# Cross attention with scores made twice: once with queries on partitions for the maximum, once with keys on partitions for the exponential, and fp32 products with the values

## The chip, the cores and the metric

The kernel runs on one core of a Trainium2 chip. The metric is the device time of one launch in microseconds (us). A core has TensorE for matrix products (PE in the profile, its weight loads PEld), VectorE (DVE), ScalarE (ACT), GpSimd (POOL) and SyncE (SP), which starts DMAs. PE writes its results to PSUM, eight banks of 2 KB on each of 128 partitions; everything else lies in SBUF. The engines run side by side and wait for one another at semaphores. PE has two clock levels, 2.4 and 1.2 GHz; the profile shows which of them was granted.

## The reference

A decoder layer on x of 64 images by 128 tokens by 128 channels: self attention, cross attention to a context of 77 keys by 96 channels, and a soft mixture of 64 experts with 32 slots, each with a residual and a layer norm. The change is in the cross attention alone, which has 16 heads of 8 channels:

```python
q = (x @ Wq).reshape(B, N, HEADS, hd).transpose(0, 2, 1, 3)
k = (context @ Wk).reshape(B, M, HEADS, hd).transpose(0, 2, 1, 3)
v = (context @ Wv).reshape(B, M, HEADS, hd).transpose(0, 2, 1, 3)
scores = jnp.einsum('bhid,bhjd->bhij', q, k) * scale
scores = jnp.where(context_mask[:, None, None, :], scores, max_neg)
attn = jax.nn.softmax(scores, axis=-1)
out = jnp.einsum('bhij,bhjd->bhid', attn, v)
out = out.transpose(0, 2, 1, 3).reshape(B, N, DIM)
return out @ Wo
...
x = _layernorm(x + _L0_xattn_ref(x, ctx_768, mask_BxS2_bf1, ...), axis=-1)
```

All values are fp32.

## The kernel before

The program is a row of stages: setup, `attention` (self attention), `attend_context` (cross attention), `prepare_slots`, `gather_slots`, `run_experts`, `mix_slots`. Each stage writes one instruction list for each engine by hand, with its own semaphores. There is no scheduler: an engine does its list in order. `steps` runs a function `step(k)` over the items, and each engine's `step` works on items k, k - 1, k - 2 and k - 3 at once, so that a stage of 32 items runs for 32 + 3 steps.

In `attend_context` an item is a pair of images, and a step has four quarters j, each for eight heads of one image (j // 2 is the image). The work for a quarter:

- Queries and keys of the pair are made once (`queries_keys`, L537 and L538), rounded to fp32r (`qkh`, L672) and the rest kept as `qkl` (L768). POOL spreads each key over four copies, each with the channels of one head only (`kbh`, `kbl`, L816). In this way a product over 32 channels gives four heads' scores side by side, 4 x 78 = 312 columns.
- `scores` (L591 to L595): two groups of four heads, each in its own 32 rows of PE's array, with three fp32r products (high by high, low by high, high by low) and one of a single row that adds the mask. Queries lie on the partitions, heads and keys on the columns.
- DVE takes the maximum over the keys of each head (L764), and `shift` (L602) subtracts it on PE by a product with the negated identity.
- ACT makes the exponential twice, in fp16 (`ph`, L699) and in fp32 (`p32`, L700), and POOL subtracts for the low part `pl` (L850).
- `turn` (L615, L616) transposes high and low part of eight heads, 16 fp16 transposes of 128 queries by 77 keys; DVE copies the high part out of PSUM (L788), ACT the low part (L690).
- `values` (L630, L631): for each head two products with the values, which were split in three bf16 parts on ACT, DVE and POOL (L676, L793, L800, L835, L840); a column of ones among them gives the sum of the exponentials.
- DVE adds the parts (L715), inverts 16 sums (L721) and multiplies (L726); PE transposes the result (L548), ACT copies it (L660), PE projects (L552), and DVE adds the residual (L731), takes the statistics (L736, L741), normalises (L746, L750), with POOL for the power (L820, L822). PE transposes again (L556), ACT and DVE keep high and low part (L664, L756).

One bank of PSUM, `psM`, serves eight small products of a step in turn. Their order, and whose reading frees the bank for the next, stands in a table that `use_bank` walks through:

```python
USES = [(queries_keys, qkl_ready, 0, None), (project, y_done, 3, 1), (own_values, v32_ready, 0, None),
        (turn_out, oT_ready, 2, 0), (project, y_done, 2, 0), (turn_x2, xl_ready, 3, 1),
        (turn_x2, xl_ready, 2, 0), (turn_out, oT_ready, 2, 1)]
```

The scores have two buffers of two banks (`psL`), the transposes one bank each, the products with the values one.

Of the kernel before, what the change touches and what calls it, by code (L numbers as in the profile page):

```python
# [18 lines left out]
ALU = mybir.AluOpType  # L19
# [25 lines left out]
C_IDENT, C_HEAD, C_END = 0, 128, 132  # L45


def constants():
    k = np.arange(128)
    c = np.zeros((128, C_END), np.float32)  # L50
    c[:, C_IDENT:C_HEAD] = np.eye(128)
    c[:, C_HEAD:C_END] = (k[:, None] % 32) // HD == np.arange(4)[None, :]
    return c
# [67 lines left out]
def setup(nc, io, w):  # L121

    with ExitStack() as ctx:
# [18 lines left out]
        def _(sync):  # L142
# [4 lines left out]
            for p in ROWS:  # L147
                sync.dma_start(w.mask[p:p + 1, :], io["mask"]).then_inc(w.mask_loaded, 16)

# [48 lines left out]
def attention(nc, io, w):  # L198
# [4 lines left out]
    with ExitStack() as ctx:  # L203
# [153 lines left out]
        def _(dve):  # L357

            dve.wait_ge(w.mask_loaded, 16 * len(ROWS))
# [87 lines left out]
def attend_context(nc, io, w):  # L447

    PAIRS = B // 2
    HW = 4 * JP
    with ExitStack() as ctx:
# [5 lines left out]
        fp = [st.sb(f"fp{i}", [128, 2, JP], BF16) for i in range(2)]  # L461
        kbh = [st.sb(f"kbh{i}", [128, 2, 4, JP], F32R) for i in range(2)]
# [5 lines left out]
        mx = [st.sb(f"mx{i}", [128, 2, 4], F32R) for i in range(2)]  # L468
        p32 = [st.sb(f"p32{i}", [128, 2, HW]) for i in range(2)]
        ph = [st.sb(f"ph{i}", [128, 2, HW], F16) for i in range(2)]  # L470
        pl = [st.sb(f"pl{i}", [128, 2, HW], F16) for i in range(2)]
        pTh = [st.sb(f"pTh{i}", [J, 8, 128], F16) for i in range(2)]
        pTl = [st.sb(f"pTl{i}", [J, 8, 128], F16) for i in range(2)]
        o9 = st.sb("o9", [128, HEADS, 9])
        orec = st.sb("orec", [128, HEADS])
        on = st.sb("on", [128, 128])
        oT = st.sb("oT", [128, 128])
# [14 lines left out]
        (qk_made, qkh_ready, qkl_ready, kbh_ready, kbl_ready, v_made, v32_ready, high_ready, rest_ready, mid_ready,  # L492
         last_ready, vs_ready) = (
            st.sem(n) for n in ("qk_made", "qkh_ready", "qkl_ready", "kbh_ready", "kbl_ready", "v_made", "v32_ready",
                                "high_ready", "rest_ready", "mid_ready", "last_ready", "vs_ready"))

        s_made, mx_ready, shifted, ph_ready, p32_ready, pl_ready, t_made, pTh_ready, pTl_ready, av_made = (
            st.sem(n) for n in ("s_made", "mx_ready", "shifted", "ph_ready", "p32_ready", "pl_ready", "t_made",
                                "pTh_ready", "pTl_ready", "av_made"))

        o_sum, o_rec, on_ready, oT_made, oT_ready, pj_made, y_done, st_done, mv_ready, ve_done, rstd_ready, x2_ready, xT_made, xh_ready, xl_ready = (
            st.sem(n) for n in ("o_sum", "o_rec", "on_ready", "oT_made", "oT_ready", "pj_made", "y_done", "st_done",
                                "mv_ready", "ve_done", "rstd_ready", "x2_ready", "xT_made", "xh_ready", "xl_ready"))
        consts_set, fp_ready = st.sem("consts_set"), st.sem("fp_ready")
        block = ctx.enter_context(nc.Block())

        def earlier(r, j, s):

            return (r, j - s) if j >= s else (r - 1, j - s + 4)


        def part(r, c):
            return vs[r.par][:, :, :, c, 0:8]
# [1069 lines left out]
```

## Time and profile before

| | us |
|---|---|
| median of 3 runs | 1877.24 (1876.05 to 1879.13) |
| the profiled execution, its span | 1877.9 |
| cross attention in it, from 191 to 757 | 566 |
| PE busy in that stretch | 494.2 |
| DVE busy | 423.5 |
| ACT busy | 348.5 |
| POOL busy | 339.6 |

The span is the time from the first to the last instruction of one execution. Busy time is the sum over an engine's instructions without overlap. A PE record lasts until its result is in PSUM, so records of products that follow each other overlap, and the distance between two starts tells what one costs. The granted clock is a share of 2.4 GHz: 1.00 is the high level throughout, 0.50 the low one throughout.

### The profile page before, as it was taken

The page shows a single profiled execution, that of the slowest core. Times are in us where ns is not written, and L with a number is a line of the kernel's source. Part 1 is how long each engine was busy: PE and PEld are TensorE (multiplying, and loading weights), DVE is VectorE, ACT ScalarE, POOL GpSimd, SP SyncE. Part 2 cuts the span into 40 slices and gives each one's busy share as a digit, 9 for nine tenths or more (in the row PEclk, how much of TensorE's full clock was granted, in tenths as well). Part 3 has the DMA queues.
Part 4 walks back from the last instruction along what each step waited for, and adds up shares of the span by engine and source line. Part 5 has one row for each costly group of instructions (what it writes and reads, how often), then busy time and mean ns, then how long its engine had stood idle before and what let it go on. Part 6 is the DMA issues. An engine that isn't in the chain of part 4 may idle for free. (4 is left out here: it accounts for less than half of the span.)

```text
span 1877.9 us, 39937 instructions
## 1 busy us (share of the span) xinstructions
PE 1659.8 (88%) x12606; PEld 1368.6 (73%) x12606; DVE 1536.8 (82%) x2882; ACT 1055.2 (56%) x2091; POOL 1307.6 (70%) x1040
## 2 busy tenths in 40 slices
PE   6775788988898898799999999879999999999997
PEld 5664577777777776577777777558888888888886
DVE  5998477778867877788888888758999999999996
ACT  2443466666656665455566555445555555555554
POOL 2333466666656655499999999817887888787887
PEclk8786688888878888899999999979999999999999
DMA  4010100000000000300000000000000000000000
GB/s 132 28 28 6 30 6 6 4 3 4 4 3 4 4 3 2 91 1 0 0 0 0 0 0 0 1 1 4 7 10 6 6 8 6 8 6 8 6 9 12
DMA packets 19980, 21.20 MB, mean 11 GB/s; under 512 B 1925, under 2 KB 14278, under 8 KB 19914
## 3 DMA queue, kind: packets, MB, share of 16 engines
q1 hardware_dynamic: 18314, 15.95, 3.1%
q0 software_dynamic: 1088, 4.19, 0.8%
q8 instruction: 35, 0.57, 0.1%
q10 hardware_dynamic: 512, 0.23, 0.0%
q14 instruction: 31, 0.25, 0.0%
HBM read 16.17 MB, written 4.19 MB: 11 GB/s over the span
## 5 line engine op out<-in xcount | busy, mean ns | idle before, releaser
L1491 POOL TENSOR_TENSOR mix_c<-mix_e,mix_rinv 128x1024 f32<-128x1024 f32 x128 | 306.9, 2397 | 151.3 <-ACT mix_rinv L1401 151.2
L1458 DVE TENSOR_REDUCE mix_sg<-mix_e 128x256 f32<-128x1024 f32 x128 | 258.5, 2019 | 43.1 <-ACT mix_e L1396 39.5
L850 POOL TENSOR_TENSOR cross_pl<-cross_p,cross_ph 128x624 f16<-128x624 f32 x128 | 175.1, 1368 | 166.0 <-ACT cross_p L700 165.9
L1064 POOL TENSOR_TENSOR gather_d<-gather_e,gather_rinv 128x1024 f32<-128x1024 f32 x128 | 245.2, 1916 | 48.9 <-DVE gather_rinv L1039 40.9
L1007 ACT ACTIVATE gather_e<-gather_L 128x1024 f32<-128x1024 f32 x128 | 131.3, 1026 | 156.5 <-PE gather_L L974 156.5
L690 ACT COPY cross_pTl<-cross_Tl 77x1024 f16<-77x1024 f16 x128 | 129.2, 1009 | 131.3 <-PE cross_Tl L616 131.3
L1029 DVE TENSOR_REDUCE gather_mx<-gather_L 128x32 fp32r<-128x1024 f32 x128 | 156.8, 1225 | 36.6 <-PE gather_L L955 30.6
L1035 DVE TENSOR_REDUCE gather_rsum<-gather_e 128x32 f32<-128x1024 f32 x128 | 156.2, 1221 | 30.9 <-ACT gather_e L1007 30.8
L1056 POOL TENSOR_TENSOR gather_dl<-gather_d,gather_dh 128x512 fp32r<-128x512 f32 x128 | 166.0, 1297 | 0.0
L1485 POOL TENSOR_TENSOR mix_cl<-mix_c,mix_ch 128x512 fp32r<-128x512 f32 x128 | 164.7, 1287 | 0.0
L1283 PE MATMUL mix_L<-kept_xh,kept_w2h 128*128 (+1 forms) x512 | 156.6, 306 | 5.9 <-DVE mix_ykl L1412 5.2
L1446 DVE TENSOR_REDUCE mix_mg<-mix_L 128x256 f32<-128x1024 f32 x128 | 154.7, 1209 | 6.9 <-PE mix_L L1285 5.1
L615 PE MATMUL cross_Th<-kept_ident,cross_ph 128*77 128x128 f16 x1024 | 159.0, 247 | 0.0
L616 PE MATMUL cross_Tl<-kept_ident,cross_pl 128*77 128x128 f16 x1024 | 158.9, 247 | 0.0
L1396 ACT ACTIVATE mix_e<-mix_L 128x1024 f32<-128x1024 f32 x128 | 131.4, 1027 | 38.0 <-PE mix_L L1294 38.0
L1284 PE MATMUL mix_L<-kept_xl,kept_w2h 128*128 (+1 forms) x512 | 145.6, 284 | 0.0
L1285 PE MATMUL mix_L<-kept_xh,kept_w2l 128*128 (+1 forms) x512 | 145.4, 284 | 0.0
L764 DVE TENSOR_REDUCE cross_mx<-cross_L 128x8 fp32r<-128x624 f32 x128 | 102.3, 799 | 44.5 <-PE cross_L L595 44.3
L616 PEld LDWEIGHTS cross_Tl<-kept_ident,cross_pl 128*77 128x77 f16 x1024 | 138.1, 138 | 0.0
L1294 PE MATMUL mix_L<-kept_neg_ident,mix_me 128*128 128x256 f32 x512 | 95.1, 308 | 46.5 <-ACT mix_me L1388 44.4
L615 PEld LDWEIGHTS cross_Th<-kept_ident,cross_ph 128*77 128x77 f16 x1024 | 135.1, 137 | 1.3 <-issue 0.3
L964 PE MATMUL slots_X<-gather_d,gather_x 128*128 128x512 f32 x256 | 134.1, 605 | 1.0 <-issue 1.0
(224 smaller groups left out, 5129.5 us busy)
## 6 DMA issues: line engine op xcount, KB each, us to landing
attn_xTg<-in_xT SPq DMA_DIRECT2D x16, 256.0 KB, 2.7
kept_xres<-in_x POOLq DMA_DIRECT2D x4, 1024.0 KB, 11.2
out<-mix_res SPq DMA_DIRECT2D x32, 128.0 KB, 1.8
cross_cg<-in_ctxT SPq DMA_DIRECT2D x32, 58.5 KB, 1.8
setup_wT<-in_w_qkvT SPq DMA_DIRECT2D x1, 192.0 KB
kept_consts<-in_consts SPq DMA_DIRECT2D x1, 66.0 KB
first_xq<-in_xq ACTq DMA_DIRECT2D x1, 64.0 KB, 2.9
setup_wproj<-in_w_proj SPq DMA_DIRECT2D x1, 64.0 KB
```

Of the source, the lines that this page charges most:

```text
L615: pe.transpose(psTh[:, h, :], ph[j % 2][:, h // 4, c], w.ident16[:])
L616: ins = pe.transpose(psTl[:, h, :], pl[j % 2][:, h // 4, c], w.ident16[:])
L850: pool.tensor_tensor(pl[j % 2][:], p32[j % 2][:], ph[j % 2][:], ALU.subtract).then_inc(pl_ready, 1)
L1029: dve.tensor_reduce(mx[j][:], psL[j][:].rearrange("p i (n s) -> p i n s", n=16), X, ALU.max)\
L1035: dve.tensor_reduce(rsum[ju][:].rearrange("p (i n) -> p i n", i=2), e[ju][:], X, ALU.add)\
L1056: pool.tensor_tensor(dl[j3][:], dd[t3.par][j3][:, 0, :], dh[j3][:], ALU.subtract)\
L1064: pool.tensor_tensor(dd[tu.par][ju][:].rearrange("p i (n s) -> p i n s", n=16), e[ju][:], rinv[ju][:].rearrange("p (i n) -> p i n", i=2).u ...
L1283: pe.matmul(o, w.w2h[:, k], w.xh[:, at], start=(c % 2 == 0), stop=False, skip_group_check=True)
L1446: dve.tensor_reduce(mg[j % 2][:], psL[j % 2][:].rearrange("p i (c t) -> p t (i c)", c=2), X, ALU.max).then_inc(mg_ready, 1)
L1458: dve.tensor_reduce(sg[j1 % 2][:], e[j1][:].rearrange("p c t -> p t c"), X, ALU.add)\
L1485: pool.tensor_tensor(cl[j5 % 2][:], cc[j5][:, 0:SPLIT, :], ch[j5 % 2][:], ALU.subtract)\
L1491: pool.tensor_tensor(cc[j3][:], e[j3][:], rinv[j3 % 2][:].unsqueeze(1).to_broadcast([128, 4, 256]), ALU.mult)\
```

## The change

The scores of a pair are still made with queries on the partitions, but only for the maximum. They are made a second time with the keys on the partitions; the negated maximum is added there, the exponential is taken once in fp32, and its output is at once the moving operand of the product with the values.

- A step has two halves b, one for each image, and the lag of the stage is 2 steps and not 3. `scores` is called for the two halves of the heads of one image, into one buffer `psS`.
- DVE writes the 16 maxima of each query so that a head's maximum lies in column 32 g + i (g is the group of four heads, i the head in it). `turn_max` is one fp32r product with the negated identity, ACT copies it to `mT`.
- `turned_scores`: 48 fp32r products of 32 rows (channels) by 77 columns (keys) as weights and 128 moving columns (queries), in the order of the four 32-row groups g, and 16 products with a 0/1 selector `pick` that add the negated maximum of each head to its scores.
- ACT: two exponentials of 77 x 1024 for each image, with the mask as a bias for each partition.
- `values` and `sums`: 16 plain fp32 products each, weights of 77 rows by 32 columns (in `vd` the eight channels of one head stand in their place and the rest is zero, in `od` ones stand there), 128 moving columns, in the order of the four 32-column groups. The output has channels on the partitions, so the transpose of the output is no longer needed.
- DVE inverts 128 x 128 sums out of PSUM and multiplies 128 x 128.
- The exponential's low part, both copies of transposes, the three-way split of the values and `shift` are gone.

```diff
-        v32 = st.sb("v32", [J, 256])
-        vr = [st.sb(f"vr{i}", [J, 256]) for i in range(2)]
-        vs = [st.sb(f"vs{i}", [J, 2, HEADS, 3, 9], BF16) for i in range(2)]
...
+        vd = [st.sb(f"vd{i}", [J, 8, 160]) for i in range(2)]
+        od = st.sb("od", [J, 160])
+        mx = [st.sb(f"mx{i}", [128, 128], F32R) for i in range(2)]
+        pick = st.sb("pick", [128, 4, JP], F32R)
+        mT = st.sb("mT", [128, 128], F32R)
+        pT = st.sb("pT", [J, 4, 4, 128])
...
-        psL = [st.ps(f"L{i}", [128, 2, 512]) for i in range(2)]
-        psTh = st.ps("Th", [J, 8, 128], F16)
-        psTl = st.ps("Tl", [J, 8, 128], F16)
-        psA = st.ps("A", [128, 512])
+        psS = st.ps("S", [128, 2, 512])
+        psP = st.ps("P", [J, 4, 4, 128])
+        psO = st.ps("O", [128, 2, 128])
...
+            def turn_max(r, b):
+                pe.wait_ge(mx_ready, r.after(4, 2 * b + 2))
+                pe.matmul(psM[:, 0:128], mx[b][:], w.neg_ident[:], start=True, stop=True).then_inc(m_made, 1)
...
+            USES = [(project, y_done, 2, 0), (queries_keys, qkl_ready, 0, None), (turn_max, mT_ready, 1, 0),
...
+            def turned_scores(r, b):
+                reach(pe, e_ready, r.after(4, 2 * b))
+                bc = slice(b * 128, b * 128 + 128)
+                for h in range(4):
+                    for n, (ks, qs) in enumerate(((kbh, qkh), (kbl, qkh), (kbh, qkl))):
+                        for g in range(4):
+                            gr = slice(32 * g, 32 * g + 32)
+                            pe.matmul(psP[:, g, h, :], ks[r.par][gr, b, h, 0:J], qs[r.par][gr, bc],
+                                      start=(h == 0 and n == 0), stop=False, skip_group_check=True)
+                pe.wait_ge(mT_ready, r.after(2, b + 1))
+                for h in range(4):
+                    for g in range(4):
+                        gr = slice(32 * g, 32 * g + 32)
+                        ins = pe.matmul(psP[:, g, h, :], pick[gr, h, 0:J], mT[gr, :], start=False, stop=True,
+                                        skip_group_check=True)
                 ins.then_inc(t_made, 1)
...
+            def values(r, b):
+                if b == 0:
+                    pe.wait_ge(vd_ready, r.after(1, 1))
+                pe.wait_ge(e_ready, r.after(4, 2 * b + 2))
+                reach(pe, oT_ready, r.after(2, b))
+                for h in range(4):
+                    for g in range(4):
+                        pe.matmul(psO[32 * g:32 * g + 32, 0, :], vd[r.par][:, 4 * b + g, 32 * h:32 * h + 32],
+                                  pT[:, g, h, :], start=(h == 0), stop=(h == 3), skip_group_check=True)
...
+                        ins = pe.matmul(psO[32 * g:32 * g + 32, 1, :], od[:, 32 * h:32 * h + 32], pT[:, g, h, :],
+                                        start=(h == 0), stop=(h == 3), skip_group_check=True)
...
+                for half in range(2):
+                    hs = slice(2 * half, 2 * half + 2)
+                    act.activation(pT[:, hs, :, :], psP[:, hs, :, :], ACT.Exp, bias=fb[r.par][:, b:b + 1])\
+                        .then_inc(e_ready, 1)
...
+                dve.reciprocal(rs[:], psO[:, 1, :]).then_inc(rs_ready, 1)
...
+                dve.tensor_tensor(oT[b][:], psO[:, 0, :], rs[:], ALU.mult).then_inc(oT_ready, 1)
```

The mask comes a second time, with keys on partitions: one more small DMA in setup on SP's queue, and one DVE instruction at the start of the self attention. POOL keeps `kbh` and `kbl` and the power, and takes over the copy of the mask row (`fp`) from ACT.

How PE's list changes. This is the list of the kernel before for one quarter (eight heads, half an image); in brackets the semaphores that an instruction waits for.

```order
L591 MATMUL cross_L<-cross_kbh,cross_qkh 128x312 [waits cross_p32_ready]
...
L595 MATMUL cross_L<-cross_fp,first_ones 128x312
...
L542 MATMUL cross_M<-first_xv,cross_cg 77x128 [waits cross_y_done]
...
L630 MATMUL cross_A<-cross_vs,cross_pTh 128x27 [waits cross_pTl_ready,cross_pTh_ready,cross_o_sum]
L631 MATMUL cross_A<-cross_vs,cross_pTl 128x18
...
L615 MATMUL cross_Th<-kept_ident,cross_ph 77x128 [waits cross_pTh_ready,cross_pTl_ready,cross_pl_ready,cross_ph_ready]
L616 MATMUL cross_Tl<-kept_ident,cross_pl 77x128
...
L602 MATMUL cross_L<-cross_mx,kept_neg_ident 128x312 [waits cross_mx_ready]
L602 MATMUL cross_L<-cross_mx,kept_neg_ident 128x312
L548 MATMUL cross_M<-kept_consts,cross_on 128x128 [waits cross_on_ready,cross_v32_ready]
```

Four such blocks make a pair; the 16 products of `values`, the 16 transposes and the two of `shift` are all that is gone from a block, the scores stay.

And this is PE's list for one whole image after the change, the second of a pair. S are the scores for the maximum, M the shared bank, O the output, P the scores with keys on partitions.

```order
L579 MATMUL cross_S<-cross_kbh,cross_qkh 128x312 [waits cross_mx_ready]
...
L583 MATMUL cross_S<-cross_fp,first_ones 128x312
...
L542 MATMUL cross_M<-first_xo,cross_oT 128x128 [waits cross_oT_ready,cross_xl_ready]
L579 MATMUL cross_S<-cross_kbh,cross_qkh 128x312 [waits cross_mx_ready]
...
L532 MATMUL cross_M<-first_xv,cross_cg 77x128 [waits cross_y_done]
...
L612 MATMUL cross_O<-cross_pT,cross_vd 32x128 [waits cross_oT_ready,cross_e_ready,cross_vd_ready]
...
L538 MATMUL cross_M<-kept_neg_ident,cross_mx 128x128 [waits cross_mx_ready,cross_vd_ready]
L619 MATMUL cross_O<-cross_pT,cross_od 32x128 x16
L546 MATMUL cross_M<-kept_consts,cross_xp 128x128 [waits cross_x2_ready,cross_mT_ready]
L594 MATMUL cross_P<-cross_qkh,cross_kbh 77x128 [waits cross_e_ready]
...
L600 MATMUL cross_P<-cross_mT,cross_pick 77x128 [waits cross_mT_ready]
L600 MATMUL cross_P<-cross_mT,cross_pick 77x128 x15
```

All of an image's work up to the next image's scores now stands in one row behind the wait for the maximum: `turn_max`, the sums, the transpose of the normalised image, 48 products with keys on partitions and 16 with `pick`. The product with the values of the image before stands ahead of `turn_max`.

DVE's list of the kernel before, for the third quarter of a step, between two maxima:

```order
L731 TENSOR_TENSOR cross_y<-cross_M,kept_xres 128x128 [waits cross_pj_made]
L736 BN_STATS cross_stats<-cross_y 128x6 [waits cross_y_done]
L715 TENSOR_REDUCE cross_o<-cross_A 128x144 [waits cross_on_ready,cross_av_made]
L740 MEMSET kept_scratch 128x1 [waits cross_st_done]
L741 BN_AGGR cross_mv<-cross_stats 128x2
L788 COPY cross_pTh<-cross_Th 77x1024 [waits cross_av_made,cross_t_made]
L793 CAST cross_vs<-cross_vr 77x32x8 [waits cross_last_ready]
L746 TENSOR_SCALAR cross_xp<-cross_y,cross_mv,cross_rstd 128x127 [waits cross_xT_made,cross_rstd_ready]
L756 TENSOR_TENSOR kept_xl<-cross_M,kept_xh 128x128 [waits cross_xh_ready]
```

Here the maxima of two different buffers alternate, with two PSUM copies and the sum of the parts among the work between them.

And after the change, from the first maximum of an image to the end of its half step:

```order
L702 TENSOR_REDUCE cross_mx<-cross_S 128x2x4 [waits cross_m_made,cross_s_made]
L718 TENSOR_TENSOR cross_y<-cross_M,kept_xres 128x128 [waits cross_pj_made]
L723 BN_STATS cross_stats<-cross_y 128x6 [waits cross_y_done]
L702 TENSOR_REDUCE cross_mx<-cross_S 128x2x4 [waits cross_s_made]
L727 MEMSET kept_scratch 128x1 [waits cross_st_done]
L728 BN_AGGR cross_mv<-cross_stats 128x2
L733 TENSOR_SCALAR cross_xp<-cross_y,cross_mv,cross_rstd 128x127 [waits cross_xT_made,cross_rstd_ready]
L737 TENSOR_SCALAR kept_xres<-cross_y,cross_mv,cross_rstd 128x128
L709 RECIPROCAL cross_rs<-cross_O 128x128 [waits cross_oT_ready,cross_av_made]
L714 TENSOR_TENSOR cross_oT<-cross_O,cross_rs 128x128 [waits cross_pj_made,cross_rs_ready]
L743 TENSOR_TENSOR kept_xl<-cross_M,kept_xh 128x128 [waits cross_xh_ready]
```

The second maximum now waits for scores that PE can only make once the first maximum has read them out of the one buffer, and the inversion of the sums stands between the residual of an image and the bank's next release (`kept_xl`).

## Rows read from the trace of the kernel before

**Rows 1.** The page: busy time of each engine, share of the span.
```profile
PE 1659.8 (88%) x12606; PEld 1368.6 (73%) x12606; DVE 1536.8 (82%) x2882; ACT 1055.2 (56%) x2091; POOL 1307.6 (70%) x1040
```

**Rows 2.** By stretch: length, busy PE, PEld, DVE, ACT, POOL, clock, DMA, GB/s.
```profile
191.00:757.00 566.00, 494.16 (x5888) 409.67 (x5888) 423.51 (x991) 348.49 (x639) 339.63 (x384) 0.83 0.02 6
...
820.00:1222.00 402.00, 392.88 (x1503) 275.95 (x1502) 335.15 (x442) 233.92 (x458) 368.92 (x237) 1.00 0.00 0
...
249.00:257.00 8.00, 7.67 (x109) 6.45 (x106) 7.42 (x21) 5.91 (x10) 5.21 (x6) 1.00 0.05 10
257.00:265.00 8.00, 6.50 (x72) 4.98 (x69) 5.20 (x12) 4.84 (x11) 5.33 (x6) 0.72 0.01 2
```

**Rows 3.** One line: count, ns (min, median, max), first and last start.
```profile
L731 DVE TENSOR_TENSOR cross_y<-cross_M,kept_xres x64: 273/277/292, 224.7 to 754.4; 128x128 f32<-128x128 f32 x64
```

**Rows 4.** Lines of the cross attention: busy us, mean ns, idle before, releaser.
```profile
L850 POOL TENSOR_TENSOR cross_pl<-cross_p,cross_ph 128x624 f16<-128x624 f32 x128 | 175.1, 1368 | 166.0 <-ACT cross_p L700 165.9
...
L690 ACT COPY cross_pTl<-cross_Tl 77x1024 f16<-77x1024 f16 x128 | 129.2, 1009 | 131.3 <-PE cross_Tl L616 131.3
L764 DVE TENSOR_REDUCE cross_mx<-cross_L 128x8 fp32r<-128x624 f32 x128 | 102.3, 799 | 44.5 <-PE cross_L L595 44.3
...
L726 DVE TENSOR_TENSOR cross_on<-cross_o,cross_orec 128x128 f32<-128x128 f32 x64 | 56.9, 890 | 0.0
L746 DVE TENSOR_SCALAR cross_xp<-cross_y,cross_mv,cross_rstd 128x127 f32<-128x127 f32 x64 | 55.4, 866 | 20.9 <-POOL cross_rstd L822 19.3
...
L816 POOL TENSOR_TENSOR cross_kbh<-cross_qkh,kept_consts 128x624 fp32r<-128x624 f32 x32 | 39.3, 1228 | 25.3 <-ACT cross_qkh L672 25.3
...
L721 DVE RECIPROCAL cross_orec<-cross_o 128x16 f32<-128x16 f32 x64 | 15.3, 239 | 0.0
```

**Rows 5.** PE in order of time, clock at 2.4 GHz: start us, busy us, line.
```profile
457.73 0.17 PE L630 MATMUL cross_A<-cross_vs,cross_pTh 77*128 77x27 bf16 x1
457.75 0.17 PE L631 MATMUL cross_A<-cross_vs,cross_pTl 77*128 77x18 bf16 x1
...
462.03 0.22 PE L615 MATMUL cross_Th<-kept_ident,cross_ph 128*77 128x128 f16 x1
462.09 0.22 PE L616 MATMUL cross_Tl<-kept_ident,cross_pl 128*77 128x128 f16 x1
...
462.55 0.27 PE L556 MATMUL cross_M<-kept_consts,cross_xp 128*128 128x128 f32 x1
462.76 0.42 PE L591 MATMUL cross_L<-cross_kbh,cross_qkh 32*128 32x312 f32 x2
463.01 0.32 PE L592 MATMUL cross_L<-cross_kbh,cross_qkl 32*128 32x312 f32 x2
463.15 0.32 PE L593 MATMUL cross_L<-cross_kbl,cross_qkh 32*128 32x312 f32 x2
463.30 0.33 PE L595 MATMUL cross_L<-cross_fp,first_ones 1*128 1x312 bf16 x2
```

**Rows 6.** PE in `run_experts`, in order of time.
```profile
1228.43 1.08 PE L1149 MATMUL slots_X<-slots_we,expert_zT 128*32 128x128 f32 x32
...
1231.76 1.04 PE L1161 MATMUL expert_T<-kept_consts,expert_xt 128*128 128x128 f32 x8
```

**Rows 7.** PE in `mix_slots`, fp32r products of 256 moving columns, in order of time.
```profile
1493.18 0.28 PE L1283 MATMUL mix_L<-kept_xh,kept_w2h 128*128 x1
1493.30 0.28 PE L1284 MATMUL mix_L<-kept_xl,kept_w2h 128*128 x1
```

**Rows 8.** From PE's keys to the low part, in order of time.
```profile
452.87 0.73 PE L538 MATMUL cross_M<-cross_cg,first_xk 96*128 96x156 f32 x2
...
453.74 0.50 ACT L672 CAST cross_qkh<-cross_M 128x412 fp32r<-128x412 f32 x1 [1.65 <-PE cross_M L538]
454.27 0.59 DVE L768 TENSOR_TENSOR cross_qkl<-cross_M,cross_qkh 128x412 fp32r<-128x412 f32 x1 [1.39 <-ACT cross_qkh L672]
```

**Rows 9.** One line: the inversion of 32 sums, ns.
```profile
L1039 DVE RECIPROCAL gather_rinv<-gather_rsum x128: 352/353/355, 775.3 to 1204.8; 128x32 f32<-128x32 f32 x128
```

More of the change, by code:

```diff
@@ L501, in attend_context @@
[L501 to L504, printed above, removed]
-        block = ctx.enter_context(nc.Block())
@@ L576, in use_bank, with scores @@
                 make(k - lag, b)
-            def scores(r, j):
-                if j == 0:
+            def scores(r, b, half):
+                if b == 0 and half == 0:
                     pe.wait_ge(fp_ready, r.after(1, 1))
@@ L633, in values, with sums @@
+            def sums(r, b):
+                for h in range(4):
+                    for g in range(4):
+                        ins = pe.matmul(psO[32 * g:32 * g + 32, 1, :], od[:, 32 * h:32 * h + 32], pT[:, g, h, :],
+                                        start=(h == 0), stop=(h == 3), skip_group_check=True)
                 ins.then_inc(av_made, 1)
@@ L667, in step @@
                 r = k - 1
-                for j in range(4):
-                    if j == 0 and k.within(PAIRS):
+                for b in range(2):
+                    r1, b1 = earlier(r, b, 1)
+                    if r1.within(PAIRS):
+                        exponentials(r1, b1)
+                    if b == 0 and k.within(PAIRS):
                         act.wait_ge(qk_made, k.after(1, 1))
-                        reach(act, shifted, (k - 1).after(4, 0))
+                        reach(act, t_made, (k - 1).after(2, 0))
@@ L701, in _ @@
-            steps(act, PAIRS, 3, step)
+                    if b == 1 and k.within(PAIRS):
+                        act.wait_ge(v_made, k.after(1, 1))
+                        reach(act, av_made, (k - 1).after(2, 0))
+                        act.copy(blocks(vd[k.par][:]), psM[0:J, 0:256].rearrange("j (c h e) -> j c h e", c=8, h=4))\
+                            .then_inc(vd_ready, 1)
+                    if r.within(PAIRS):
+                        keep_max(r, b)
+                    if (k - 2).within(PAIRS):
+                        keep_high(k - 2, b)
@@ L703, in _ @@
+            steps(act, PAIRS, 2, step)
         @block.vector
@@ L759, in step @@
                 r = k - 1
[L760 removed]
+                for b in range(2):
+                    r1, b1 = earlier(r, b, 1)
                     if r.within(PAIRS):
[L762 to L766 removed]
+                        peak(r, b, 0)
+                    if (k - 2).within(PAIRS):
+                        add_residual(k - 2, b)
+                        statistics(k - 2, b)
+                    if r.within(PAIRS):
+                        peak(r, b, 1)
+                    if (k - 2).within(PAIRS):
+                        aggregate(k - 2, b)
+                    if b == 0 and k.within(PAIRS):
@@ L808, in _ @@
-            steps(dve, PAIRS, 3, step)
+                    if (k - 2).within(PAIRS):
+                        normalise(k - 2, b)
+                        keep_residual(k - 2, b)
+                    if r1.within(PAIRS):
+                        invert_sums(r1, b1)
+                        divide(r1, b1)
+                    if (k - 2).within(PAIRS):
+                        low_part(k - 2, b)
+            steps(dve, PAIRS, 2, step)
         @block.gpsimd
```

284 lines of the change are left out of this document (88 added, 196 removed).

## The prediction

> **What bounds the kernel now.** I read the page's busy times first [rows 1]: PE 88% and DVE 82%. The change touches one stage, so the stretches by stage come next [rows 2]: the cross attention takes 566 us, with PE busy 494, DVE 424, ACT 348 and POOL 340 us, and a granted clock of 0.83. No engine is full. The step between two images' residuals [rows 3] is (754.4 - 224.7) / 63 = 8.41 us, so a pair takes 16.8 us; 32 pairs are 538 us and 28 us are filling and draining. The rows by line [rows 4] show DVE at its maximum (L764) and two operations that are longer than their size: L726 and L746 take 0.89 and 0.87 us for 128 x 128 elements, as if they waited while POOL's L850 and L816 ran (1.37 and 1.23 us). PE records overlap; the order of time [rows 5] gives what a product costs. So the pair is a chain that goes round PE, DVE, ACT and POOL, and PE at the low clock.
>
> **What goes.** In each pair: four of L850 on POOL (5.5 us), four of L690 and four of eight exponentials on ACT, four of L788 on DVE, the adding and the slow L726. On PE, 64 transposes of 0.06 us [rows 5] and 64 small products go, with 8 of `shift`. ACT falls to about half and POOL to kbh, kbl and the power. Neither was full, so this gives time only as far as the new chain is shorter. It has to be added up, since one buffer of scores now ties the engines in a row.
>
> **Prices on PE, at the high clock.** [Rows 5]: two row groups of scores run side by side; a round of both costs 0.14 to 0.15 us (463.01, 463.15, 463.30), the first of four 0.25. L556 is followed after 0.21 us where 0.11 is its own column time, so a change of tiling costs 0.10. Four rounds: 0.68, with the change 0.78. [Rows 6]: 32 records of plain fp32 with 32-column weights take 1.08 us. Each of 16 products is two records, and four column groups run side by side: (1.08 - 0.27 for the last record's length) / 7 = 0.116, so 8 rounds cost about 0.88; L1161's 8 full-width records give (1.04 - 0.27) / 7 = 0.11 each. This is the form of the new `values` and `sums`: 0.98 each with the change of tiling. From end of columns to result: 0.22 - 0.05 = 0.17 [rows 5], and about 0.1 to wake the next engine (0.03 from L672 to L768, up to 0.14 from PE to L672) [rows 8].
>
> **The unknown price.** `turned_scores` is 64 fp32r products of 128 moving columns for each image, 16 rounds of four row groups. No row shows fp32r with fewer than 256 columns. From below: 256 columns cost 0.12 a product [rows 7], 312 cost 0.14 [rows 5], which is columns / 2.4 GHz and 0.011 to 0.015 more, so 128 columns would cost 0.07. From above: plain fp32 needs two records of 0.11 [rows 6], 0.22 a round. Below 0.07 nothing speaks. I take 0.07, since the nearest rows are of the same type: 16 rounds are 1.12, with tiling change and first weights 1.34 us.
>
> **The reciprocal.** 16 elements take 0.239 [rows 4], 32 take 0.353 [rows 9]: 7.1 ns an element. 128 are 0.353 + 96 x 0.0071 = 1.04 us. It runs beside turned_scores, and delays what stands behind it on DVE: divide, the bank's release (`kept_xl`) and the next maximum.
>
> **The new chain, high clock.** From the first maximum of an image to that of the next.
> First image: maximum 0.80, wake 0.10, scores 0.78, queries and keys 0.81 (2 x 412 columns at 0.11 for 128, and a change), result and wake 0.27, qkh 0.50, 0.03, qkl 0.59, wake 0.10, turn_max 0.20, sums 0.98, transpose 0.21, turned scores 1.34, the next scores 0.60, result and wake 0.27: 7.58.
> Second image: 0.80 + 0.10 + 0.78, own values 0.54, values 0.98, turn_max 0.20, sums 0.98, a wait for the normalised image (POOL's power and L746's successor) 0.30, 0.21 + 1.34 + 0.60 + 0.27: 7.10.
> Together 14.7 us. The exponentials (2 x 1.01 by L690's row) lie beside scores and q/k. DVE adds 0.4: kbh and kbl stand on POOL where DVE normalises, as L746 shows now. So 15.1 us a pair against 16.8.
>
> **The clock.** The PE terms of the two chains are 4.9 and 5.6 us; at the low clock they double and a pair takes about 24.5 us (some waits are swallowed). The clock is 1.00 in stretches in which PE is busy 7.67 of 8 us and 0.72 where it is 6.50 of 8 [rows 2]. Before, 0.83 means the low level for 34% of the time. In PE's columns, before fills about 70% of a pair: scores 3.1 (four times 0.78), 64 transposes 3.7, 64 small products at 0.025 1.6, `shift` 1.1 (8 x 312 columns), the shared bank's products about 2.4: 12 of 16.8 us [rows 5]. After it is 10.5 and 1.6 that lie beside the chain, of 15.1: 80%. At 95% and more (820 to 1222) the low level is absent. Between 70% (0.34) and 95% (0), 80% gives 0.20. A pair takes 1 / (0.8 / 15.1 + 0.2 / 24.5) = 16.3 us.
>
> **The sum.** (16.3 - 16.8) x 32 = -16 us. The lag is one step shorter; of the 28 us of filling and draining I take off 12 (between 0 and one pair's 16.8). Together -28 us. The mask's DMA and one operation in setup: up to 1 us, hidden or not. The profiled execution has 1877.9 us of span, 0.7 over the median of 1877.24, so the forecast is 1849 us.
>
> The Trainium skill, "TensorE: Matmul & The Clock Gate", Back-to-back issue gap, speaks against 0.07: with its own weight load a product of 128 columns keeps a sustained spacing of about 81 ns, and its part on packing small matmuls measured 3.07 and not 4 for four row groups. By both, 64 x 0.081 / 3.07 = 1.69 for 1.12, an estimate. The transposes here, with 77-column weights of their own, start 0.06 apart, below that figure; four row groups no row shows. The sum would be about 1885.
>
> **Rivals.**
> (B) Weight loads or a weaker overlap make a round of turned scores 0.12, as a 256-column product costs [rows 7]. For: each product has its own 77 columns of weights, and nothing hides them behind 53 ns of columns. Against: the transposes [rows 5]. Price: 32 rounds x 0.05 = 1.6 a pair at the high clock: 16.7, with 15% at the low level (27 there) 17.7: +29 - 12: 1894.
> (C) fp32r at 128 columns runs no faster than plain fp32. Place: turned_scores, behind the wait for the maximum, where the whole chain waits. Price: 0.15 x 32 = 4.8 a pair; 19.9 less 0.5 that the PE backlog hides, 19.5; with 5% at the low level (34 there) 19.9: +99 - 12: 1965. It decides from a round of about 0.10 us on: there the pair passes 17.2 and the shorter lag is eaten up. For: this kernel's fp32r products are all 256 columns or wider, all its 128-column products plain fp32. Against: from 512 to 256 columns the extra hardly changes. This is the case that ends slower.
> (D) The clock sinks, because the one score buffer makes PE wait in each image. Half of the time low: 1 / (0.5 / 15.1 + 0.5 / 24.5) = 18.7: +61 - 12: 1926; for it, 0.72 at 81% busy [rows 2].
> (E) Four row groups don't run side by side (the change doesn't do what its order is for): 64 x 0.07 = 4.5 for 1.12, 6.7 a pair, 32 x 6.7 over the forecast: 2063. Against: two groups do [rows 5], four column groups do [rows 6].
> (F) The clock stays high: 15.1 a pair, -54 - 12: 1811. For it: 1.00 in the denser stretch of the same stage [rows 2].
> For (F) speaks also the Trainium skill, same page, PE-mode transpose: transposes don't count as busy for the clock, and 64 of them go. Whether that is so here no row separates from the waits; by that rule the time would be 1811.
>
> **How the numbers follow.** Forecast 0.37, B 0.15, C 0.25, D 0.12, E 0.03, F 0.08. The forecast's own range is 1825 to 1880. Overall 1805 to 1985: below lies 0.04, above E and a third of C. A measurement of this kernel tells 0.2% (3.8 us) from no change. Faster by more than 0.2%: 0.28 of the forecast, 0.03 of B, 0.08 of F, 0.03 of D, 0.42. Within: 0.09. Slower: 0.49, more than faster although the likeliest single case is a gain, because rivals with a price add up on that side.
>
> **What would show it.** Right: residual steps of about 8.1 us; PE records of cross_P that start four within 0.07 to 0.08 us; values and sums near 0.9 us a block; a reciprocal near 1.04 us; granted clock of the stage 0.88 to 0.92; the stage from 191 to about 729. Wrong: four starts of cross_P 0.12 or more apart (B, 0.22 for C); clock under 0.8 (D); a single row group at a time (E). DVE's reciprocal over 1.3 us, or normalisations of 1.2 us, would put DVE's list in the chain and add 0.3 to 1 us a pair.

## The result: slower by 12%, with TensorE's clock at its low level in the whole stage

The kernel after takes 2101.5 us (median of 4 runs, 2099.1 to 2103.0) against 1877.1: a ratio of 1.120, interval 1.118 to 1.121. Its profiled execution has a span of 2097.2 us and a mean clock of 0.787. The forecast was 1849 in a range of 1805 to 1985; the time lies above the range.

The cross attention by stretch (length, busy PE, PEld, DVE, ACT, POOL, clock, DMA, GB/s), and the start of the residual's additions, first and last:

```profile
191.00:979.00 788.00, 742.76 (x9728) 558.71 (x9728) 337.55 (x735) 196.84 (x319) 136.28 (x255) 0.50 0.02 4
```
```profile
L718 DVE TENSOR_TENSOR cross_y<-cross_M,kept_xres x64: 279/292/293, 219.6 to 976.5; 128x128 f32<-128x128 f32 x64
```

Against [rows 2] the stage has grown from 566 to 788 us, by 222; the two spans differ by 2097.2 - 1877.9 = 219.3, so the loss is in this stage. PE is busy for 94% of it, and its granted clock is 0.50, the 1.2 GHz level, throughout; before it was 0.83. A step between residuals is (976.5 - 219.6) / 63 = 12.0 us against 8.41 [rows 3], a pair 24.0 against 16.8. DVE went from 424 to 338 us, ACT from 348 to 197, POOL from 340 to 136: the work left these engines as planned, and they now wait for PE. The costliest lines of the stage (busy us, mean ns, idle before, releaser):

```profile
L612 PE MATMUL cross_O<-cross_pT,cross_vd 77*32 77x128 f32 x2048 | 123.9, 421 | 1.5 <-ACT cross_pT L654 1.5
L619 PE MATMUL cross_O<-cross_pT,cross_od 77*32 77x128 f32 x2048 | 123.8, 420 | 0.0
...
L579 PE MATMUL cross_S<-cross_kbh,cross_qkh 32*128 32x312 f32 x256 | 81.0, 610 | 36.6 <-issue 20.8 <-DVE cross_mx L702 15.0 <-POOL cross_kbl L777 0.8
```
```profile
L702 DVE TENSOR_REDUCE cross_mx<-cross_S 128x8 fp32r<-128x624 f32 x128 | 103.4, 808 | 241.9 <-PE cross_S L583 241.9
L709 DVE RECIPROCAL cross_rs<-cross_O 128x128 f32<-128x128 f32 x64 | 61.3, 958 | 122.4 <-PE cross_O L619 122.4
L737 DVE TENSOR_SCALAR kept_xres<-cross_y,cross_mv,cross_rstd 128x128 f32 (+1 forms) x64 | 49.5, 773 | 0.0
L733 DVE TENSOR_SCALAR cross_xp<-cross_y,cross_mv,cross_rstd 128x127 f32<-128x127 f32 x64 | 39.0, 609 | 31.6 <-POOL cross_rstd L783 31.6
```

DVE sits idle 242 us for scores and 122 us for sums; PE itself waits 15 us for the maximum and 21 us for "issue". Values and turned scores, PE in order of time (start us, busy us, line), at the low clock:

```profile
501.29 1.94 PE L612 MATMUL cross_O<-cross_pT,cross_vd 77*32 77x128 f32 x32
503.16 0.48 PE L538 MATMUL cross_M<-kept_neg_ident,cross_mx 128*128 128x128 f32 x1
...
506.03 0.34 PE L594 MATMUL cross_P<-cross_qkh,cross_kbl 32*77 32x128 f32 x4
506.15 0.34 PE L594 MATMUL cross_P<-cross_qkl,cross_kbh 32*77 32x128 f32 x4
506.29 0.34 PE L594 MATMUL cross_P<-cross_qkh,cross_kbh 32*77 32x128 f32 x4
506.42 0.34 PE L594 MATMUL cross_P<-cross_qkh,cross_kbl 32*77 32x128 f32 x4
```

Values take 1.94 us. Of the turned scores four row groups start together, and the next four follow 0.13 us later.

### The profile page after: what moved, and what is told of

Same layout as the page of the kernel before. It is cut to its first block and busy times, and to the rows that moved or that the text cites. A ratio compares the mean times of both kernels' runs of the same rounds, so it can differ in the third digit from the quotient of the medians.

```text
span 2097.2 us, 45892 instructions
## 1 busy us (share of the span) xinstructions
PE 1898.6 (91%) x16446; PEld 1509.4 (72%) x16446; DVE 1453.4 (69%) x2630; ACT 902.5 (43%) x1771; POOL 1103.8 (53%) x912
## 5 line engine op out<-in xcount | busy, mean ns | idle before, releaser
L781 POOL TENSOR_TENSOR cross_veps<-cross_mv,kept_eps 128x1 f32<-128x1 f32 x64 | 12.2, 190 | 614.9 <-DVE cross_mv L728 614.9
L702 DVE TENSOR_REDUCE cross_mx<-cross_S 128x8 fp32r<-128x624 f32 x128 | 103.4, 808 | 241.9 <-PE cross_S L583 241.9
L654 ACT ACTIVATE cross_pT<-cross_P,cross_fb 77x1024 f32<-77x1024 f32 x128 | 135.1, 1105 | 129.0 <-PE cross_P L600 129.0
L709 DVE RECIPROCAL cross_rs<-cross_O 128x128 f32<-128x128 f32 x64 | 61.3, 958 | 122.4 <-PE cross_O L619 122.4
L1266 PE MATMUL mix_Y<-mix_c,kept_phi 128*128 128x256 f32 x512 | 131.7, 380 | 0.0
L612 PE MATMUL cross_O<-cross_pT,cross_vd 77*32 77x128 f32 x2048 | 123.9, 421 | 1.5 <-ACT cross_pT L654 1.5
L619 PE MATMUL cross_O<-cross_pT,cross_od 77*32 77x128 f32 x2048 | 123.8, 420 | 0.0
```

Source lines behind the costliest of these rows:

```text
L1266: ins = pe.matmul(psY[:], w.yk[:, 4 * j + c, :], cc[j][:, c, :], start=False, stop=(j == 3 and c == 3))
```

## The experiments

Three words are used below. A product is *row-grouped* when its weights fill 32 of PE's 128 rows and others run beside it (first scores two groups, turned scores four). It is *column-grouped* when they fill 32 of the columns (values and sums, four groups), and *whole* when it is neither. A *filler* is a product whose result nobody uses. The clock of a run is that of the stretch 250 to 500 us; where a row is shown, it is this stretch in the columns of [rows 2]. All but the last run, which was repeated five times, are single; before, run beside them, took 1873.6 to 1883.9 us. Before and after stand there as:

```profile
250.00:500.00 250.00, 221.87 (x2693) 184.69 (x2694) 194.91 (x458) 159.56 (x294) 155.21 (x178) 0.85 0.02 4
```
```profile
250.00:500.00 250.00, 238.30 (x3135) 179.23 (x3123) 109.16 (x236) 63.98 (x103) 42.64 (x80) 0.50 0.02 4
```

### Which products hold the clock down

Seven kernels issue some of the row- or column-grouped products whole, in the same number of rounds. They leave out a part of the terms (three quarters in values, sums and turned scores), so they are there for their time alone. Three edits, alone and together:

```
 values, sums ("values whole"):
-    for g in range(4): pe.matmul(psO[32*g:32*g+32, 0, :], vd[r.par][:, 4*b+g, 32*h:32*h+32], pT[:, g, h, :], ...)
+    pe.matmul(psO[:, 0, :], vd[r.par][:, 4*b+h, 0:128], pT[:, h, h, :], ...)          # sums alike
 turned scores ("turned whole"):
-    for g in range(4): pe.matmul(psP[:, g, h, :], ks[r.par][gr, b, h, 0:J], qs[r.par][gr, bc], ...)
+    pe.matmul(psP[:, n, h, :], ks[r.par][:, b, h, 0:J], qs[r.par][:, bc], ...)        # pick, mT alike
 first scores ("first whole"):
-    for i in range(2): (qkh, kh), (qkl, kh), (qkh, kl) on rows gr, fill on one row, into psS[:, i]
+    (qkh, kh), (qkl, kh) into psS[:, 0], (qkh, kl) into psS[:, 1], on all rows; fill still on one row, into psS[:, 1]
```

Values whole: 

> This kernel issues values and sums as 4 products each on the whole array (128 columns of weights) instead of 4 rounds of four column groups, and leaves out 3/4 of their terms; the number of rounds and their length stay. The turned scores stay on four row groups. My theory: products on 32-row or 32-column groups count for less in what grants the clock than products on the whole array, and after has almost nothing else. Theory 1a (the column groups are what holds the clock down): granted clock of the stage from 0.50 up to 0.9 or more, time 1811 to 1860. Theory 1b (both forms weigh): the clock rises only in part, 0.55 to 0.8, time 1880 to 2050. Rival 2 (the turned scores alone hold it down) and rival 3 (the pauses of PE in each image hold it down, whatever the form of the products): 0.50, 2085 to 2105.

Turned whole: 

> This kernel issues the turned scores as 12 and 4 products of 128 rows instead of 12 and 4 rounds of four row groups (3/4 of the terms left out, the exponent scaled so that values stay finite); rounds and their length stay. Values and sums stay on column groups. Theory 1a (column groups hold the clock down): 0.50 and 2085 to 2105. Theory 1b (both forms weigh): 0.55 to 0.8, 1880 to 2050; the turned scores are 32 of 64 rounds of an image, so it should rise about as much as in the kernel with whole values. Rival 2 (the turned scores alone): 0.9 or more, 1811 to 1860. Rival 3 (the pauses): 0.50, 2085 to 2105.

Both: 

> Both edits at once: values, sums and turned scores as the same number of rounds of products on the whole array. Theory 1 in all its forms: granted clock 0.95 or more in the stage, residual steps of 7.5 us, 1811 (between 1800 and 1850). Rival 3 (the pauses of PE): PE waits as often as in after, so 0.50 and 2085 to 2105; the time would then be that of after to 1%.

All three: 

> As the kernel with both edits, and the first scores too are issued as products of 128 rows (4 for 4 rounds). Theory 1: if the first scores' row groups matter, this one has a higher clock than the one with both edits, up to 1.00 and 1811; if that one is already at 1.00, no difference over 10 us. Rival 3: 0.50 and 2085 to 2105 as before.

First whole: 

> Of the kernel after only the first scores are changed: 4 products of 128 rows for each half instead of 4 rounds of two row groups (part of the terms left out), same number of rounds. So far the stage stood at 0.50 with values, turned scores or both on the whole array (2058, 2075, 2025 us) and at 0.94 when the first scores were whole too (1791). Theory 4 (all whole-array work counts together, and the clock rises once it is most of what PE does; no one place decides): 0.50 and 2070 to 2100 here. Theory 5 (the first scores, which fill only two of four row groups, are what holds the clock down): 0.9 or more and 1790 to 1860.

First and values: 

> First scores, values and sums on the whole array, the turned scores alone on four row groups. By time at the high clock the whole-array part is about 3.5 of 5 us of PE's work for an image. Theory 4 (whole-array work counts together): between 0.5 and 0.94, so 0.6 to 0.9 and 1830 to 2000; Theory 5 (the first scores decide): 0.9 or more and 1790 to 1850.

First and turned: 

> First scores and turned scores on the whole array, values and sums on four column groups. Theory 4: 0.6 to 0.9 and 1830 to 2000, as with values and first scores whole. Theory 5: 0.9 or more and 1790 to 1850.

| whole | us | clock, 250 to 500 |
|---|---|---|
| none (after) | 2101.5 | 0.50 |
| values | 2057.6 | 0.50 |
| turned | 2075.1 | 0.50 |
| values, turned | 2025.1 | 0.51 |
| first | 2117.5 | 0.50 |
| first, values | 2054.2 | 0.50 |
| first, turned | 1807.5 | 0.99 |
| all three | 1791.4 | 0.97 |

The row of first and turned whole, and its residual line:

```profile
250.00:500.00 250.00, 226.88 (x3318) 172.36 (x3318) 182.14 (x396) 106.13 (x173) 72.87 (x138) 0.99 0.02 5
```
```profile
L711 DVE TENSOR_TENSOR cross_y<-cross_M,kept_xres x64: 278/280/292, 221.1 to 684.7; 128x128 f32<-128x128 f32 x64
```

PE's pauses are not the cause. With first and turned whole PE waits longer for the maximum than in after (27.8 us for 15.0), at twice the clock:

```profile
L575 PE MATMUL cross_S<-cross_kbh,cross_qkh 128*128 128x312 f32 x128 | 51.4, 401 | 28.6 <-DVE cross_mx L695 27.8 <-POOL cross_kbl L770 0.8
```

In this order of work, with nothing added, either row-grouped part alone is enough to hold about 0.50 (four runs), and only with both whole does the clock rise; the form of the column-grouped values and sums changes little with either (0.50 and 0.50, 0.99 and 0.97). That it is not fp32r follows from the same runs, since the whole products are fp32r as well.

None of the theories came out as I put them. Theory 1 in all its forms expected 0.95 with values, sums and turned scores whole; the clock stood at 0.51. Theory 5 expected that the first scores decide; alone they left 0.50. Theory 4 expected 0.6 to 0.9 with first and values whole, and it was 0.50.

The number of row-grouped rounds doesn't decide alone either. With values and turned whole the stage has the same 8 rounds of two row groups an image as the kernel before, which stands at 0.85, and yet:

```profile
250.00:500.00 250.00, 244.04 (x1289) 213.37 (x1288) 122.56 (x266) 70.63 (x115) 49.08 (x93) 0.51 0.01 3
```

What else of the new order counts, these runs don't show. Nor do they separate the row-grouped rounds from the changes of tiling before and behind them.

The times at 0.50 differ in part for another reason: after, "values" and "first" have the stops at the end of PE's loop that are treated below, the others have none. With turned whole the time, 2075.1, is that of after with a short loop, 2077.3.

The residual's steps with first and turned whole are (684.7 - 221.1) / 63 = 7.36 us, 14.7 a pair with the slow start in it and 14.4 in the middle of the stage. This is the new chain at the high clock, in a kernel with fewer products; for after 15.1 was forecast.

The same edit of the first scores in the kernel before: 

> The kernel before with its scores issued as 4 products of 128 rows for a step instead of 4 rounds of two row groups (part of the terms left out), same number of rounds. Theory W (row-grouped rounds are what holds the clock down, in before as in after): clock of the stage 0.95 or more, pairs of 16.0, 1850 (1835 to 1860). Rival (something that only the kernel after has decides): 0.83 and 1870 to 1885.

```profile
250.00:500.00 250.00, 216.82 (x2565) 180.44 (x2564) 202.83 (x476) 166.59 (x308) 161.75 (x185) 0.90 0.02 4
```

1850.3 us beside 1874.4 for before, clock 0.90 for 0.85: the time came out as expected, the clock rose less than expected. The mean clock of the whole execution is 0.936, against 0.914 to 0.922 in all runs of before beside the experiments, so the form of the first scores seems to count in the old order too, but it is only a part of what holds the clock down there. This is one run, and it leaves out terms.

### Adding whole products to the kernel after

All of after's work is kept; a helper adds products of the 16-bit identity with itself, 256 columns:

```
+def fill_in(n, out, moving, start=True): for _ in range(n): pe.matmul(out, w.ident16[:], moving, start=start, ...)
     reach(pe, mx_ready, ...)                +    fill_in(4, psS[:, 0, 0:256], same)
     reach(pe, e_ready, r.after(4, 2*b))     +    fill_in(4, psP[:, 0, 0:2, :], same)
+    fill_in(4, psP[:, 0, 0:2, :], zero[:], start=False)
     pe.wait_ge(mT_ready, ...)
```

> The kernel after, all of its work kept, with 16 added products for each image on the whole array (16-bit, 256 columns, 0.11 us each at the high clock, 0.21 at the low): 4 before each half of the first scores, 4 before the turned scores, 4 (of zeros, added to them) before the wait for the transposed maximum. Theory 4: the added work is 1.76 us of whole-array work for an image at the high clock; if that is enough the stage goes to 0.8 or more and the pair to 15.1 + about 2.5 us that aren't hidden, 1890 (1850 to 1950). Theory 5: the first scores stay on two row groups, so 0.50, the pair grows by about 32 x 0.21 = 6.8 us and the time is 2101 + 218 = 2320 (2250 to 2330).

```profile
250.00:500.00 250.00, 229.15 (x3714) 162.54 (x3710) 116.36 (x254) 69.34 (x112) 46.72 (x88) 0.85 0.02 5
```

2065.6 us, outside the 1850 to 1950 of theory 4. The clock rose as theory 4 says (theory 5 falls), with all of after's products kept, but pairs at the high clock took 19.1 us and the fillers ate most of the gain. This run shows the turned scores at the high clock, four row groups every 0.07 us:

```profile
411.13 0.24 PE L603 MATMUL cross_P<-cross_qkh,cross_kbl 32*77 32x128 f32 x4
411.20 0.24 PE L603 MATMUL cross_P<-cross_qkl,cross_kbh 32*77 32x128 f32 x4
411.27 0.24 PE L603 MATMUL cross_P<-cross_qkh,cross_kbh 32*77 32x128 f32 x4
```

### The stops at the end of PE's loop

PE's waits in after, 300 to 900 us (total, times, longest), and the instruction queue's DMA, 300 to 600 us (packets, MB, share), of after and then of before:

```profile
PE cross_S L579 <- issue: 20.8, 6, 3.6
```
```profile
q8 instruction: 36, 0.59, 0.8%
```
```profile
q8 instruction: 4, 0.07, 0.1%
```

Six times, 98 us apart, which is four pairs and one turn of PE's loop, PE stands still with nothing to wait for. The loop made shorter: 

> The kernel after with PE's loop two pairs long instead of four; nothing else. In after PE stands still for 3.4 to 4.0 us at the end of each turn of its loop, six times, with nothing that it waits for but issue. Theory L (the long loop body, not a wait, makes these stops): they go, 6 x 3.8 less 0.2 each that passes anyway: 2101 - 22 = 2079 (2070 to 2085), clock still 0.50. Rival: the stops have another cause (they then come twice as often or stay) : 2100 or more; or they are what keeps the clock down, and it rises above 0.6.

```
-            steps(pe, PAIRS, 2, step)
+            steps(pe, PAIRS, 2, step, unroll=2)
```
```profile
250.00:500.00 250.00, 245.46 (x3234) 184.70 (x3226) 112.24 (x243) 64.77 (x106) 45.23 (x86) 0.50 0.01 3
```
```profile
L718 DVE TENSOR_TENSOR cross_y<-cross_M,kept_xres x64: 280/292/292, 221.7 to 956.3; 128x128 f32<-128x128 f32 x64
```
```profile
q8 instruction: 2, 0.03, 0.0%
```

2077.3 us: the stops and the instruction traffic are gone, for 24 us, and the clock didn't move although PE is now busy for 98% of the time. A pair takes 2 x (956.3 - 221.7) / 63 = 23.3 us. This fits a loop whose body after had to fetch anew in every turn. The Trainium skill says of this ("Runtime: NRT & Kernel Launch", Instruction fetch mechanics) that a taken branch to a target outside the pages held stalls until the page has come by DMA; the queue's 36 packets against 4 and 2 agree.

With fillers too: 

> The kernel with 16 whole-array fillers for each image, with the short loop. With the long loop it had pairs of 19.1 us at the high clock and of 23 to 29 after each of the six stops. Theory: a stop of 3.5 us drops the clock and it takes long to come back; without stops the clock stays at 1.00 from some 60 us into the stage, pairs of 19.1 throughout: 32 x 19.1 + 30 for start = 641 us of stage, 1955 (1940 to 1975). Rival (the clock falls by itself at this load): still 0.80 to 0.85, 2040.

2069.2 us at 0.80: this theory fell, and the rival has the clock right and the time 29 us too low. Without stops the clock still changes between its levels (the longest high stretches are 51 to 62 us, the low ones 10 or 11 us and three times 41). Two versions with fewer fillers, in which the first scores have their high part alone:

```
-                    pe.matmul(out, qkl[r.par][gr, bc], kh_, start=False, stop=False)
-                    pe.matmul(out, qkh[r.par][gr, bc], kl_, start=False, stop=False)
```

> A version meant for use. Short loop; the first scores, from which only a maximum is taken, made from the high parts alone (2 products and the fill go: 8 rounds of two row groups for an image become 4); 8 fillers for an image: 4 after values in a spare part of their bank, 2 before the turned scores, 2 before the wait for the maximum. If the clock holds: pairs of 14.4 (measured at the high clock with first and turned scores whole) less 1.5 for the shorter first scores plus 1.4 for fillers that nothing hides = 14.3, and 1810 (1790 to 1850), faster than before and after. If the clock doesn't hold with so few fillers: pair 24.0 - 2.1 + 3.4 = 25.3 and no stops: 2120; in between if it alternates.

> As the version with 8 fillers, with only the 4 after values. If the clock holds: pair 13.6, 1785. If it doesn't: pair 24.0 - 2.1 + 1.7 = 23.6, less the stops, 2065. I think it less likely to hold (0.4) than the one with 8 (0.6), since less of PE's time is whole-array work.

Both stayed at 0.50, at 2132.4 and 2054.7 us, within 13 us of the bad branch of each expectation. I had given the better branch 0.6 and 0.4.

### Do transposes count?

Fillers as fp32 transposes and as fp32 products of the same 128 x 128 identity, in after with the short loop:

```
-                    pe.matmul(out, w.ident16[:], moving, ...)
+                    pe.transpose(out, w.ident, w.ident)      # or pe.matmul(out, w.ident, w.ident, start=True, stop=True)
```

8 transposes for an image: 

> The kernel after with the short PE loop (2077) and 8 added transposes for an image (fp32, 128 x 128, two records of 0.11 us each at the high clock), 2 before each half of the first scores and 4 before the turned scores. Rule T (transposes count for nothing in the clock): 0.50, and the time grows by 64 x 8 x 0.43 = 220 less little: 2290 (2270 to 2300). If transposes count as products do: as the kernel with the same number of products.

8 products: 

> The same places and the same number of added instructions, as ordinary fp32 products of the identity with itself, 128 x 128. They take 1.76 us an image at the high clock, as the 16 fillers of 16 bits did (2069 with the short loop). Theory W: 0.75 to 0.85 and 2040 to 2100. If only the kind of data or the number of instructions matters and fp32 products don't help: 0.50 and 2290.

16 transposes: 

> The kernel after with the short loop and 16 added fp32 transposes for an image, in the places of the 8 added products that gave 0.96 and 1979 us. At the low clock 16 x 0.21 us = 3.4 us an image. Rule T (transposes count for nothing): about 0.5, as with 8, and 2197 + 64 x 8 x 0.21 = 2305 (2280 to 2320). If they count as products of the same length do: 0.75 or more and 1980 to 2070.

Their rows in this order:

```profile
250.00:500.00 250.00, 244.30 (x2925) 178.24 (x2922) 96.29 (x210) 57.55 (x92) 38.37 (x72) 0.53 0.01 3
```
```profile
250.00:500.00 250.00, 231.12 (x4215) 184.04 (x4213) 133.86 (x289) 77.21 (x126) 53.96 (x101) 0.96 0.02 4
```
```profile
250.00:500.00 250.00, 232.97 (x4086) 180.81 (x4087) 129.15 (x282) 76.15 (x123) 51.18 (x98) 0.91 0.01 4
```

2197.1, 1979.5 and 1971.6 us. A transpose is one record and a product two, so 8 transposes took half the PE time of 8 products, and the clock hardly rose (0.53); at the same PE time they raise the clock (0.91) nearly as products do (0.96). The products gained more than I expected, and 16 transposes came out at the other end from rule T. With the products all of after's work is done and the clock is high: so a high clock in this stage needs neither terms left out nor other data. What the Trainium skill says ("TensorE: Matmul & The Clock Gate", PE-mode transpose), that transposes don't count as busy for the clock, doesn't agree with these fp32 ones; for the 16-bit ones that the change removes no run shows it.

### A version that beats both

The kernel before, with whole products in the place where PE waits 0.65 us a pair for `vs`:

```
-                if j == 0:
-                    pe.wait_ge(vs_ready, r.after(1, 1))
                 if j % 2 == 0:
                     reach(pe, o_sum, r.after(2, j // 2))
+                if j == 0:
+                    for _ in range(5):
+                        pe.matmul(psA[:, 0:256], w.ident16[:], <ident16 twice>, start=True, stop=True)
+                    pe.wait_ge(vs_ready, r.after(1, 1))
```

> The kernel before with 5 added whole-array products (16-bit, 256 columns, 0.11 us at the high clock) for each pair, in the bank of the values, where PE waits 0.65 us a pair for vs. Theory W (whole-array work holds the clock up, row-grouped rounds don't): before changes between the levels every few us (1.00 for 10 to 14 us, 0.50 for 3 to 7), so a little more whole-array work should lengthen the high stretches: clock of the stage from 0.83 to 0.87 or more, 1855 to 1872. If the fillers only take PE's time: 0.83 and 1880 to 1890.

```profile
250.00:500.00 250.00, 215.52 (x2846) 178.19 (x2844) 199.26 (x466) 163.34 (x301) 159.39 (x181) 0.95 0.03 6
```
```profile
PE cross_L L591 <- issue: 18.9, 5, 4.0
```
```profile
q8 instruction: 39, 0.64, 0.9%
```

1856.9 us (before 1874.4) at 0.95, and now this loop, 20 products longer, shows the same stops and instruction traffic. With `unroll=2` for PE: 

> The kernel before with 5 whole-array fillers a pair and PE's loop two pairs long instead of four. With the long loop it was 1857 us, with five stops of 3.9 to 4.4 us in PE for which nothing is named but issue; pairs without one took 15.3 us. Theory L (the stops come from the length of the loop's body): none are left, 5 x 4.1 = 20 us and the drops of the clock after them go: 1857 - 20 - 5 = 1832 (1825 to 1842), clock of the stage 0.95 or more. If the stops stay: 1855 to 1860.

```profile
250.00:500.00 250.00, 222.75 (x2964) 183.81 (x2961) 208.27 (x486) 169.75 (x315) 166.10 (x189) 0.96 0.02 4
```
```profile
PE cross_L L591 <- issue: 3.8, 10, 0.4
```

1840.5 us (5 runs, 1836.7 to 1841.7); ratio to before 0.980, interval 0.978 to 0.981. The long stops are gone (longest 0.4 us), for 16 us of the 25 expected. Before with the short loop alone has no run; it had no such stops to lose.

## Why the prediction was wrong

**The step that failed is the clock.** Its sentence was "Between 70% (0.34) and 95% (0), 80% gives 0.20". The measured share at the low level is 1.00. My price of a pair at that level was 24.5 us, and 32 pairs at 24.5 instead of 16.3 make 1849 + 262 = 2111, against 2101.5. That this comes so near is partly luck: a pair took 24.0 us with the stops and 23.3 without them, so the price was about 1.2 too high, and the 24 us of stops, which the sum didn't hold, filled most of the gap. In the runs, after without the stops takes 2077.3 us and with both row-grouped parts whole 1807.5: 270 us, most of it the clock.

The term failed in its premise: I counted every column of PE alike. In the new order row-grouped work didn't hold the clock up as whole work did (0.50 against 0.99 in the same rounds). The change raises it from 8 rounds an image to 24, while the 64 transposes, 64 small products and `shift` of a pair that leave were none of them row-grouped. How much each of these counts is not shown: 8 rounds stood at 0.85 in the old order and at 0.51 in the new. I also drew a line between two busy shares, 70% and 95%; after stands at 0.50 with 94%.

**What was right.** The round of four row groups at 0.07 us; B, C and E, which held 0.43 of the chance, are refuted by it. The estimate that I made from two figures of the Trainium skill ("TensorE: Matmul & The Clock Gate", Back-to-back issue gap; Measured speedup vs the span model), 1.69 us for 16 rounds, doesn't agree with it either: 16 x 0.07 is 1.12 (the second figure, 3.07, is the skill's for 512 columns; here there are 128). The chain at full clock, 15.1, is about right, but no run has after alone at that level: the kernel with fewer products took 14.4 and that with 16 fillers 19.1, less 2 x 16 x 0.11 for them 15.6 (an estimate). Case F's 1811 lies near the 1807.5 of first and turned whole, which is that other kernel. The reciprocal, 1.04, is 0.96 us. Values and sums: 1.94 us at the low clock for 0.98 at the high one. ACT and POOL fell as said.

**Case D** had the mechanism's name, a sinking clock, but not its cause nor its size: it blamed PE's waits and gave half the time at the low level, 1926. Its evidence, 0.72 at 81% busy, was the pattern of before. I should have asked what an all-low stage costs: 2111 by my own prices, outside my range.

**Not foreseen:** 24 us of the loss are the stops of a loop body that the short products made longer: PE has about 9728 / 32 = 304 records a pair, before had 5888 / 32 = 184.

**Left open:** why 8 row-grouped rounds an image hold 0.51 in the new order and 0.85 in the old; whether the rounds or the changes of tiling count; how much whole work is enough (16 fillers of 16 bits gave 0.80, 8 fp32 products of the same PE time 0.96; four of the former multiply zeros and they stand elsewhere); whether 16-bit transposes count; whether a version of after that computes the turned scores whole and in full would pay: it needs keys masked for 16 heads and not for 4, so four times the elements of L777.

## What to carry to other kernels

Products on 32 rows side by side are fast by columns (0.07 us for four of 128) but in this stage did not hold TensorE's clock up: before replacing whole-array work by them, price the stage at both clock levels, and treat "all low" as a case of its own. If PE waits somewhere for another engine, a few idle whole-array products there can pay (5 a pair gave 0.9% in one run, and 2.0% with the shorter loop). After any edit that lengthens an unrolled loop, look at PE's "issue" waits and the instruction queue: 4 us a turn here, cured by a shorter body.

## What the runs showed of the hardware

PE busy for 94% of 788 us stood at 0.50 throughout (98% of 250 us with the short loop); busy for 91% with other forms of product it ran at 0.99. Two kernels with the same rounds on PE and without stops, 24 rounds an image of them in a different form, differ by 270 us (2077.3 and 1807.5). 16 fp32 transposes added to an image raised the clock from 0.50 to 0.91, nearly as 8 fp32 products of the same PE time did (0.96). Twenty more products in a loop of four pairs took the instruction queue from 4 packets to 39 in 300 us, with five stops of up to 4.0 us.
